# Bias of the second up projection: added by VectorE in four passes over 128 columns in place of a product on TensorE

## What is computed

```python
# hidden_states: the normalised tokens, 256 features; Wg, Wu: 256 x 1024; Wd: 1024 x 256
mlp = jax.nn.silu(hidden_states @ Wg + bg) * (hidden_states @ Wu + bu) @ Wd + bd
return mlp + experts_states
```

## Time and profile before

| | us |
|---|---|
| median of three runs | 1509.58 |
| lowest, highest run | 1504.55, 1510.39 |
| the profiled execution, its own time | 1507.87 |
| span of its trace | 1506.1 |
| from VectorE's `csum` of one unit to that of the next | 38.82 to 38.96 |

### The profile page before, as it was taken

One profiled execution on the slowest core, in us unless ns is written; L12 is line 12 of the kernel. 1 busy time (PEld: TensorE's weight loads), 2 busy tenths in 40 slices (PEclk: granted clock), 3 DMA queues, 4 the chain that ended last, 5 costly groups with the idle time before them and its releaser, 6 DMA issues. The chain is left out here.

```text
span 1506.1 us, 43877 instructions
## 1 busy us (share of the span) xinstructions
PE 1420.1 (94%) x14960; PEld 1044.1 (69%) x14960; DVE 1187.8 (79%) x4544; ACT 928.4 (62%) x1684; POOL 919.1 (61%) x845
## 2 busy tenths in 40 slices
PE   6899679999999999999999999999999999999978
PEld 4566447777777777777777777777777777777657
DVE  5444288888888888888888888898888888888812
ACT  3766336666666666666666666666666666666641
POOL 4655356666666666666666666666666666666620
PEclk8999879999999999999999999999999999999989
DMA  6556942221111122222111122212222222222027
GB/s 186 205 183 211 274 73 53 52 51 45 47 45 47 50 51 51 51 51 50 47 46 46 47 50 49 48 48 51 51 51 51 51 51 51 65 51 53 9 95 234
DMA packets 217147, 113.74 MB, mean 76 GB/s; under 512 B 128872, under 2 KB 211224, under 8 KB 217112
## 3 DMA queue, kind: packets, MB, share of 16 engines
q1 hardware_dynamic: 216304, 112.88, 27.3%
q10 hardware_dynamic: 808, 0.42, 0.2%
HBM read 73.08 MB, written 40.16 MB: 75 GB/s over the span
## 5 line engine op out<-in xcount | busy, mean ns | idle before, releaser
L1150 POOL TENSOR_TENSOR sumxy<-xy 128x1024 f32<-128x1024 f32 x128 | 240.7, 1901 | 0.0
L1393 DVE TENSOR_REDUCE bmax<-q_bank 128x32 f32<-128x512 f32 (+3 forms) x512 | 219.9, 481 | 16.5 <-PE q_bank L1633 15.4
L1240 ACT ACTIVATE pts<-k_bank 128x512 f32<-128x512 f32 (+2 forms) x384 | 177.4, 490 | 42.0 <-PE k_bank L1668 41.2
L1494 DVE SCALAR_TENSOR_TENSOR mw<-sumxy,c,ex 128x1024 f32<-128x1024 f32 x128 | 176.0, 1394 | 1.5 <-issue 0.8
L1633 PE MATMUL q_bank<-ko,qo 96*128 96x512 bf16 (+3 forms) x512 | 142.9, 306 | 24.6 <-DVE bmax L1393 22.6
L1116 POOL TENSOR_TENSOR pad<-pad 128x1 f32<-128x1 f32 x32 | 6.2, 193 | 256.4 <-DVE top L1412 256.4
L1615 PE MATMUL f_bank<-xt,wfu 128*128 128x128 f32 x1024 | 162.3, 281 | 0.0
L1174 POOL TENSOR_TENSOR cw<-cw,mw 128x1024 f32<-128x1024 f32 x64 | 150.8, 2356 | 6.6 <-ACT mw L1264 1.6
L1615 PE MATMUL f_bank<-xt,wfg 128*128 128x128 f32 x1024 | 150.3, 279 | 0.0
L1615 PEld LDWEIGHTS f_bank<-xt,wfu 128*128 128x128 f32 x1024 | 139.4, 191 | 11.5
L1264 ACT ACTIVATE mw<-mw,erec 128x1024 f32<-128x1024 f32 x128 | 145.7, 1139 | 0.0
(11 more groups left out here) (211 smaller groups left out, 3340.1 us busy)
## 6 DMA issues: line engine op xcount, KB each, us to landing
qo<-s_qs SPq DMA_DIRECT2D x192, 64.0 KB, 2.2
ko<-s_ks SPq DMA_DIRECT2D x186, 64.0 KB, 2.2
s_qs<-parts SPq DMA_DIRECT2D x8, 768.0 KB, 4.7
s_ks<-parts SPq DMA_DIRECT2D x8, 768.0 KB, 6.3
s_v<-vo SPq DMA_DIRECT2D x8, 544.0 KB, 3.0
vv<-s_v SPq DMA_DIRECT2D x32, 136.0 KB, 2.3
vw<-s_v SPq DMA_DIRECT2D x64, 68.0 KB, 2.5
xin<-in_L_attn_x_dram SPq DMA_DIRECT2D x8, 512.0 KB, 6.9
```

Of the source, the lines that this page charges most:

```text
L1150: done("sum_done", g_.tensor_tensor(sumxy[:, h, :, :], xy[:, 0, h, 0:XK, None].broadcast_to([P, XK, KEYS]), xy[:, 1, h, None, :].broadcast ...
L1240: last = s.activation(pts[:, h, OFFS[j]:OFFS[j] + n], bank[:, 0:n], ACT.Exp)
L1393: last = v.tensor_reduce(bmax[:, i, h, 0:n], Q.bank(job)[:, o:o + n * BLK].rearrange("p (n j) -> p n j", j=BLK), AX.X, ALU.max)
L1494: done("mw_done", v.scalar_tensor_tensor(mw[:, h, :], sumxy[:, h, :, :].rearrange("p a b -> p (a b)"), c8[:, h, 7:8], ex[:, h % 2, :], ALU ...
```

## The change

The bias product of `u0` and `u1` is gone; the first of the eight products of the bank now starts the sum (`start=True`) for its own 128 columns. A new tile `bias_u` holds `bu` with the hidden feature within a block of 128 on the partition, and the block's number along the row; it is loaded by one DMA on SyncE's queue behind `bdb`, of 128 x 8 single numbers. VectorE's `up(t, j)` is now four instructions over 128 columns each, `(PSUM + bias) * hidden`, with the bias as a column pointer; the semaphore that frees the bank is raised by the last of them. The gate's bias keeps its product. The three-part staging of the biases in the first stage is halved to `bg` alone.

Besides, three pairs of semaphores that GpSimd raises one after the other (`strike_done` and `pc_in`, `xy_done` and `cand_done`, `e8_in` and `nmax_done`) are merged into one each, counted to two per unit. No instruction moves for it, and each waiter waits for the same instruction as before.

```diff
@@ -199,9 +199,10 @@
-        bias3 = sb("bias3", [96, 2, 2, P], BF16)
+        bias3 = sb("bias3", [96, 2, P], BF16)
         tile_of = sb("tile_of", [96, 4, P], BF16)
         bdb = sb("bdb", [P, C])
+        bias_u = sb("bias_u", [P, FT])
...
                 for r in range(3):
-                    for a, src in enumerate((fbg, fbu)):
-                        act.dma_start(b1[32 * r:32 * r + 4, a, :, :],
-                                      src.rearrange("(j k p) -> k j p", j=2, k=4)).then_inc(bias_in, 16)
+                    act.dma_start(b1[32 * r:32 * r + 4, :, :],
+                                  fbg.rearrange("(j k p) -> k j p", j=2, k=4)).then_inc(bias_in, 16)
...
                 sp.dma_start(bdb[:, :], fbd.rearrange("(o n) -> o n", o=1).broadcast_to([P, C])).then_inc(units_in, 16)
+                sp.dma_start(bias_u[:, :], fbu.rearrange("(f p) -> p f", p=P), allow_slow_non_contiguous=True).then_inc(units_in, 16)
...
                     F.wait_read(dve, t, f"g{j}")
                     F.wait_full(dve, t, f"u{j}")
-                    F.released(f"u{j}", v.tensor_tensor(hidden(j), hidden(j),
-                                                        F.bank(f"u{j}")[:, :], ALU.mult))
+                    for k in range(4):
+                        f = 4 * j + k
+                        last = v.scalar_tensor_tensor(hT[:, f, :], F.bank(f"u{j}")[:, P * k:P * k + P], bias_u[:, f:f + 1],
+                                                      hT[:, f, :], ALU.add, ALU.mult)
+                    F.released(f"u{j}", last)
...
-                    w_, kind = (wfg, 0) if name == "g" else (wfu, 1)
+                    w_ = wfg if name == "g" else wfu
                     if k == 0:
                         F.wait_free(pe, t, f"{name}{j}")
-                        mm(F.bank(f"{name}{j}")[:, :], bias3[:, kind, j, :], tile_of[:, :, :].rearrange("r k t -> r (k t)"),
+                    if k == 0 and name == "g":
+                        mm(F.bank(f"{name}{j}")[:, :], bias3[:, j, :], tile_of[:, :, :].rearrange("r k t -> r (k t)"),
                            start=True, stop=True)
                     o = P * (4 * j + k)
                     dst = F.bank(f"{name}{j}")[:, k * P:k * P + P]
                     for c in range(2):
-                        last = mm(dst, w_[:, c, o:o + P], xt[:, t.half, c, :], start=False, stop=(c == 1),
+                        last = mm(dst, w_[:, c, o:o + P], xt[:, t.half, c, :], start=(name == "u" and c == 0), stop=(c == 1),
                                   skip_group_check=True)
```

More of the change, by code:

```diff
@@ L269, in build @@
             dn = sb("dn", [P, EX // P, C])
[L270 to L273, removed]
+            b1 = sb("b1", [96, 2, P])
+            b2 = sb("b2", [96, 2, P])
+            b3 = sb("b3", [96, 2, P], BF16)
+            b4 = sb("b4", [96, 2, P], BF16)
             bank = [ps(f"sbank{i}", [P, 512]) for i in range(4)]
@@ L390, in _ @@
                 statistics(dve, 1)
[L391 to L397, removed]
+                dve.wait_ge(bias_in, 3 * 16)
+                ch.link(v.tensor_copy(b3[:, :, :], b1[:, :, :]))
+                v.tensor_copy(bias3[0:32, :, :], b3[0:32, :, :])
+                ch.link(v.tensor_tensor(b2[:, :, :], b1[:, :, :], b3[:, :, :], ALU.subtract))
+                ch.link(v.tensor_copy(b4[:, :, :], b2[:, :, :]))
+                v.tensor_copy(bias3[32:64, :, :], b4[32:64, :, :])
+                v.tensor_tensor(bias3[64:96, :, :], b2[64:96, :, :], b4[64:96, :, :], ALU.subtract)
                 statistics(dve, 2)
@@ L1110, in _ @@
                 pool.wait_ge(constants, 8)
-                pool.wait_ge(units_in, 16 * 6)
+                pool.wait_ge(units_in, 16 * 7)
                 def pad_wait():
@@ L1120, in selection @@
                     pad_wait()
-                    done("strike_done", g_.tensor_copy(strike[:, :, :, 0:4], top[:, :, :, 0:4]))
+                    done("strike_pc", g_.tensor_copy(strike[:, :, :, 0:4], top[:, :, :, 0:4]))
                     if now:
                         K.wait_full(pool, now, "pcT")
-                    done("pc_in", g_.tensor_tensor(pc[:, :, :, :], lc[:, :, :, 0:NB],
+                    done("strike_pc", g_.tensor_tensor(pc[:, :, :, :], lc[:, :, :, 0:NB],
                                                    top[:, :, :, 0:1].broadcast_to([P, TT, HG, NB]), ALU.subtract))
@@ L1144, in candidates @@
                     need(pool, "xy_in", t)
-                    done("xy_done", g_.tensor_tensor(xy[:, :, :, :], xy[:, :, :, :], sim[:, :, :, :], ALU.add))
-                    done("cand_done", g_.tensor_tensor(cand[:, :, :, :], t8[:, 0, :, :, None].broadcast_to([P, PH, 8, 8]),
+                    done("xy_cand", g_.tensor_tensor(xy[:, :, :, :], xy[:, :, :, :], sim[:, :, :, :], ALU.add))
+                    done("xy_cand", g_.tensor_tensor(cand[:, :, :, :], t8[:, 0, :, :, None].broadcast_to([P, PH, 8, 8]),
                                                        t8[:, 1, :, None, :].broadcast_to([P, PH, 8, 8]), ALU.add))
-                    need(pool, "xy_done", t)
+                    need(pool, "xy_cand", t, 1)
                     for h in range(PH):
@@ L1155, in candidates @@
                             need(pool, "c8_done", t)
-                            done("e8_in", g_.tensor_tensor(e8[:, :, :], c8[:, :, :], c8[:, :, 0:1].broadcast_to([P, PH, 8]),
+                            done("e8_nmax", g_.tensor_tensor(e8[:, :, :], c8[:, :, :], c8[:, :, 0:1].broadcast_to([P, PH, 8]),
                                                            ALU.subtract))
-                            done("nmax_done", g_.tensor_scalar(nmax[:, :], c8[:, :, 0], -1.0, None, ALU.mult))
+                            done("e8_nmax", g_.tensor_scalar(nmax[:, :], c8[:, :, 0], -1.0, None, ALU.mult))
                 def last_expert(t):
@@ L1478, in best_pairs @@
                 def best_pairs(t):
-                    need(dve, "cand_done", t)
+                    need(dve, "xy_cand", t)
                     pad_wait(8)
```

20 lines of the change are left out of this document (10 added, 10 removed).

## The result

The changed kernel is slower by about one per cent:

| | before | after |
|---|---|---|
| median, us | 1509.57 (4 runs) | 1523.12 (4 runs) |
| lowest, highest | 1504.55, 1510.39 | 1520.00, 1525.38 |
| ratio after/before, 95% interval | | 1.0095 [1.0066, 1.0124] |
| profiled execution, own time; span | 1507.87; 1506.1 | 1520.00; 1518.3 |
| csum to csum, mean of the full units (lowest, highest) | 38.93 (38.83, 38.97) | 39.37 (39.27, 39.41) |

A forecast was written before the change was run, and what follows sets the result against it. The prediction took a ring between VectorE and GpSimd, 38.82 us a unit, as the bound; 31 x 0.44 = 13.6 us for the first `up`, all else nothing, added to 1507.87 gave 1521.5 us, own range 1515 to 1527, with rivals 1509 to 1532.

The forecast's parts named there:

- the ring of VectorE and GpSimd: `csum` to end of `at`, 1.08 us to the first `mw`'s end, VectorE to next `csum`: 38.82 us a unit, TensorE outside.
- The price of `up(t, 0)`, +0.44 us: Between `mw` and `csum`, four passes take 1.05 us against 0.61, paid in full in 31 units: 13.6 us.
- scaling `mw` down: Pass time from `mw`, 1024 wide with a pointer, less 0.95 us for 896 columns: 0.25 to 0.26 us a pass.
- The lower bound without a pointer: From a PSUM reduction of 128 x 128, 0.282 us less 0.08 overlap: 0.20 us a pass, 0.81 for four.
- TensorE's 0.15 us a product counted at nothing: Each bias product removed saves TensorE 0.15 us, 9.6 us in 64, but only lengthens its wait at the block maxima.
- the cover of `up(t, 1)`: Second `up`, outside the ring: loses 0.59 us against 1.25 us of VectorE's waits at last maxima and local scores; costs nothing.
- The load, the staging, the merged semaphores at nothing: Before the unit stage: `bias_u` load 0, at most +2 us; halved staging 0, at most 1 us gained; semaphores 0.
- TensorE setting the end (1): Rival: TensorE bounds the kernel after all, so 64 products save 9.6 us, 1498.3 us; chance 0.08.
- The free pointer (2): Rival: VectorE's passes pipeline as closely as the reduction, +0.20 us a unit, 6.2 us, 1514.1 us; chance 0.19.
- Its milder form: GpSimd's list 0.1 us shorter a unit by meeting VectorE's two-input instructions in better order: 3 to 4 us less.
- No overlap (3): Rival: VectorE's passes do not overlap, +0.76 us a unit, 23.6 us, 1531.4 us; chance 0.07.
- Passes held by GpSimd (4): Rival: GpSimd's sums hold the passes through the SBUF pointer, +2.5 to 3 us a unit, 1593 us; chance 0.04.

The follow-up runs named there:

- 6: Changed kernel with GpSimd's addition of `bdb` to `xb` done for one column of 256: 1509.41 us, 1.0001 against the kernel before.
- 3: Changed kernel with `up` as one pass over 512 columns, bias products still gone, up projection's bias left out: 1508.53 us, 1.0006 against the kernel before.
- 4: Changed kernel with the constant 0.5 in place of the pointer to the bias column, four passes kept: 1514.14 us, 1.0042 against the kernel before.
- 8: Changed kernel with VectorE's `csum` moved ahead of the key marks: 1512.08 us, 1.0024 against the kernel before.
- 2: Kernel before with only `u1` treated as in the change, `u0` keeping its product and single pass: 1508.81 us, 1.0001 against the kernel before.
- 5: Kernel before with both halves in four passes and the bias products kept, bias added twice: 1523.26 us, 1.0104 against the kernel before.
- 10: Kernel before with `csum` ahead of the key marks, `up(t, 0)` behind the second head's maxima, `gate(t, 1)` behind the third head's and `unselected`: 1482.31 us, 0.9829.
- 12: On top of 11, key marks moved behind the third head's maxima and best pairs behind the fourth head's: 1536.91 us, 1.0180 against the kernel before.
- 1: Kernel before with only `u0` treated as in the change, `u1` keeping its product and single pass: 1521.82 us, 1.0097 against the kernel before.
- 7: Kernel before with VectorE's `csum` moved ahead of the key marks: 1497.98 us, 0.9931 against the kernel before.
- 11: Changed kernel with `csum` ahead of the key marks, `up(t, 0)` behind the second head's maxima, `gate(t, 1)` behind the third head's and `unselected`: 1492.35 us, 0.9907.

## Why the prediction was right, and where not

- **The bound: the ring of VectorE and GpSimd.** Right, but for one reading: GpSimd does not work "without a pause" from `csum` to `at`. It waits 0.11 us for `smax_hi` in three units of four, for a cast that its own `pc` holds up. No run tests what this is worth. 6 shortens GpSimd's side by 0.47 us and the unit by 0.43; 3 shortens TensorE's list by 64 products and the unit by nothing.
- **The price of `up(t, 0)`, +0.44 us.** Right: 1.05 us for four passes, 0.258 us apart (said: 0.25 to 0.26) and 0.342 long (said: 0.33), by scaling `mw` down. The lower bound without a pointer, 0.20 us a pass, is what 4 measured. The unit grew by 0.44 us; 31 such would be 13.6 us, and 12.1 us were measured between the profiled executions, 13.55 between the medians.
- **That the price fits to the hundredth is luck.** The scaling as it is written gives 1.20 - 0.95 = 0.248 us a pass, 0.99 us for four and +0.38 us, 11.8 us in 31 units; it was rounded up to 0.26 and to 1.05 us. The form of the instruction and the size of the pointer's part are what the rows carried, not the last 0.06 us.
- **That the exact sum fits is partly chance.** The unit in which the loop is left lost 0.95 us more than its passes, and the last stage gained 2.2 us, 1.7 of them by a load that lands sooner in every kernel with `bias_u`. Neither was foreseen.
- **TensorE's 0.15 us a product counted at nothing.** The size (0.14) and the conclusion are right. The step failed where I worked out the cover of `up(t, 1)`: "against it VectorE loses here only its own 0.44 us and the 0.15 us that TensorE gains at `u1`". TensorE gains nothing at `u1`: a wait of the same length appears at the third head's maxima (14.32 us over the stretch in both traces). So the products that VectorE waits for behind `up(t, 1)` come no earlier: in the unit shown, the last maxima start 5.76 us and the local scores 10.06 us behind `csum` in both traces. VectorE pays its 0.44 us and not 0.59, and all of it ahead of the last maxima, in small waits there (the one before them fell from 0.33 to 0.23 us, in total from 15.4 to 8.1) and by an `up` that starts 0.1 us sooner behind `csum`. The wait for the local scores, which was said to shrink, stays as it was, 0.92 and 0.93 us in the unit shown and 29 us in all. It made no difference here. In the expectation for 8 it made the whole: a gain was counted that the next wait took back.
- **`up(t, 1)` is covered.** Right (2), and with more room than was said: `up` now ends 0.32 us ahead of the down projection's third part (832.25 against 832.57), where 0.05 us had been left to it.
- **The load, the staging, the merged semaphores at nothing.** Right within what the traces show up to the first unit: -0.38 us at TensorE's first product, +0.35 us at the first `csum`. Within the units nothing shows: experiment 3, which has all three, stands at 38.92 us. Only the last stage's 1.7 us go with the load.
- **Rivals.** TensorE setting the end (1) is refuted by 3, 5 and 6. The free pointer (2) is refuted by 4, which is the kernel that it describes: 6.2 us were said for it, 6.4 were measured (1514.14 against 1507.75 on that chip), and the changed kernel costs twice as much. Its milder form did not occur: from `csum` to the end of `at` are 17.79 us in the mean before and 17.78 after. No overlap (3): 0.26 us apart and not 0.34. Passes held by GpSimd (4): none lasts over 0.352 us. Of the two rules of the Trainium skill that were weighed, the formula of "VectorE: DVE Perf Modes" (section on the trn2 errata) gave +0.47 us for an `up`, as an estimate, and +0.44 was measured; but that is near by chance. The formula knows no pointer, and without one 4 measured +0.20. It gives the length of a pass well (0.69 us for 512 columns, measured 0.69; 0.29 for 128, measured 0.28 with a constant), but what four passes cost is the distance from start to start, 0.198 us. The key point of "GPSIMD Engine Reference" in the Trainium skill says "two SBUF inputs" and nothing on pointers. The passes have one tensor in SBUF, one in PSUM and the pointer in SBUF, and ran undisturbed beside GpSimd, so the pointer did not count as the second input.

## What to carry to other kernels

Find the ring before you price an edit: where two engines wait for each other in turn, check which instruction ends at a constant distance behind one of another engine, and then price only what lies in the ring; test it by shortening the other engine's part. An engine at 94% gains nothing from fewer instructions while its next meeting with a later engine stands where it was; look at the first wait behind the saving. To let it gain, put what it waits for first on the other engine's list (10 gained 25 us without any less work), but follow each moved result to every reader, or the list of a third engine pays for it (12).

## What the runs showed of the hardware

- A VectorE pass over 128 x 128 that reads PSUM and SBUF starts 0.198 us behind the one before with a constant as its scalar (4), and 0.258 us with a column in SBUF: 0.06 us for a pointer. One pass over 128 x 512 takes 0.61 us; four over 128 x 128 take 0.81 us without and 1.05 us with the pointer.
- A VectorE pass with both tensors in SBUF, started beside a GpSimd addition of the same kind, ended 1.08 us behind that addition in every unit, whether it had lasted 1.44 or 1.84 us (1 to 6 and 12, with the kernels before and after); the same pass takes 1.27 us undisturbed. In 7 to 11, where GpSimd waits in between, the distance is 1.08 to 1.39 us and the pass 1.28 to 1.52.
- A VectorE cast over 128 x 16 (`smax_hi`, float32 to bfloat16, all in SBUF) that ran into a GpSimd addition over 128 x 512 (`pc`) lasted 0.48 us, or 0.62 in 6, and ended 0.03 us behind it; in all other units it lasted 0.17 or 0.18 us.
- Taking away a 512-column bfloat16 product ahead of float32 ones saves 0.14 us and not the 0.22 us by which its record led the next: before, the next weights were loaded beneath it.
